# Paged attention, one core: the new-value products of four heads joined into one of 512 columns on a diagonal, and the row maximum taken as a minimum of scaled scores

## The reference

```python
kc = k_cache[block_table].reshape(bsz, L, HK, D)      # 64 sequences, L = 512 cached keys
vc = v_cache[block_table].reshape(bsz, L, HK, D)      # 8 key heads of D = 128
k_all = jnp.concatenate([kc, k], axis=1)              # 32 new tokens behind them
v_all = jnp.concatenate([vc, v], axis=1)
k_all = jnp.repeat(k_all, 4, axis=2)                  # 4 query heads share a key head
v_all = jnp.repeat(v_all, 4, axis=2)
scores = jnp.einsum('bqhd,bkhd->bhqk', q, k_all) * SCALE
scores = jnp.where(valid[:, None, None, :], scores, -1e+30)
probs = jax.nn.softmax(scores, axis=-1)
o = jnp.einsum('bhqk,bkhd->bqhd', probs, v_all)
```

## Time and profile before

| what | value |
|---|---|
| time, median of 3 runs | 3394.45 us (3389.18 to 3395.66) |
| the profiled execution, its own time | 3397.83 us |
| its span, first to last instruction | 3396.0 us |
| mean granted TensorE clock | 0.986 |
| attention stage | about 1630 to 2870 us of the span |

### The profile page before, as it was taken

One profiled execution on the slowest core, in us unless ns is written; L12 is line 12 of the kernel. 1 busy time (PEld: TensorE's weight loads), 2 busy tenths in 40 slices (PEclk: granted clock), 3 DMA queues, 4 the chain that ended last, 5 costly groups with the idle time before them and its releaser, 6 DMA issues. The chain is left out here.

```text
span 3396.0 us, 69875 instructions
## 1 busy us (share of the span) xinstructions
PE 3284.2 (97%) x22398; PEld 3029.0 (89%) x22398; DVE 2326.7 (69%) x6644; ACT 1764.6 (52%) x4307; POOL 1330.0 (39%) x2391
## 2 busy tenths in 40 slices
PE   7799999999899999999899999999999999999999
PEld 5688899987778888888899999999999998888878
DVE  6445544445478787878899999989999996423274
ACT  4323222233327788788666666666666666322222
POOL 0231100000007878888666666656666653100002
PEclk9899999999999999999999999999999999999999
DMA  5422422334545555556766666656666666533353
GB/s 206 135 58 71 127 82 80 86 104 144 199 151 176 173 172 177 183 178 202 238 219 219 213 219 221 219 182 219 214 220 219 222 224 192 178 103 109 115 183 103
DMA packets 448054, 571.96 MB, mean 168 GB/s; under 512 B 171657, under 2 KB 330185, under 8 KB 430794
## 3 DMA queue, kind: packets, MB, share of 16 engines
q1 hardware_dynamic: 427978, 429.08, 40.3%
q0 software_dynamic: 19712, 138.42, 11.6%
HBM read 394.60 MB, written 172.75 MB: 167 GB/s over the span
## 5 line engine op out<-in xcount | busy, mean ns | idle before, releaser
L2625 PE MATMUL l2a_x<-l2a_pt,l2a_V 128*128 128x128 f32 x4096 | 542.3, 275 | 1.0 <-DVE l2a_pn L2559 1.0
L2625 PEld LDWEIGHTS l2a_x<-l2a_pt,l2a_V 128*128 128x128 f32 x4096 | 498.5, 192 | 1.4 <-issue 1.4
L2535 DVE CUSTOM_DVE_ANT_0 l2a_sm<-l2a_s,l2a_B 128x544 f32<-128x544 f32 x512 | 367.9, 719 | 69.3 <-PE l2a_s L197 66.1
L2489 ACT ACTIVATE l2a_p<-l2a_sm,l2a_st 128x544 f32<-128x544 f32 x512 | 380.1, 742 | 27.4 <-DVE l2a_st L2538 27.2
L2344 POOL CAST l2a_K<-cache 128x256 fp32r x768 | 304.2, 447 | 228.6 <-issue 228.6
L2344 POOL CAST keys<-cache 128x256 fp32r x750 | 299.2, 451 | 179.4 <-issue 149.0
L2475 ACT ACTIVATE l2a_pt<-l2a_t 128x512 f32<-128x512 f32 x512 | 305.6, 597 | 101.7 <-PE l2a_t L2608 101.6
L2608 PE MATMUL l2a_t<-ident,l2a_p 128*128 128x128 f32 x2048 | 307.4, 273 | 5.4 <-ACT l2a_ao L2482 5.4
L2549 DVE TENSOR_SCALAR l2a_p<-l2a_p,l2a_st 128x512 f32<-128x512 f32 x512 | 275.6, 538 | 18.2
L2482 ACT ACTIVATE l2a_ao<-l2a_x 128x128 f32<-128x128 f32 x512 | 142.3, 278 | 280.6 <-PE l2a_x L2626 280.5
L197 PE MATMUL l2q_pa<-keys,cache 128*128 128x512 f32 (+1 forms) x1024 | 267.1, 343 | 3.4 <-DVE head L143 3.4
(11 more groups left out here) (856 smaller groups left out, 8672.3 us busy)
## 6 DMA issues: line engine op xcount, KB each, us to landing
s_qT<-l2q_qo SPq DMA_DIRECT2D x128, 512.0 KB, 2.8
head<-s_qT SPq DMA_DIRECT2D x64, 512.0 KB, 5.8
l2a_Q<-s_qT SPq DMA_DIRECT2D x64, 512.0 KB, 5.4
s_ao<-l2a_ao SPq DMA_DIRECT2D x64, 512.0 KB, 6.2
l2o_a<-s_ao SPq DMA_DIRECT2D x128, 256.0 KB, 3.1
s_kn<-l2q_ko SPq DMA_DIRECT2D x128, 128.0 KB, 2.9
head<-s_kn SPq DMA_DIRECT2D x32, 512.0 KB, 5.8
wqraw<-in_wqkv SPq DMA_DIRECT2D x32, 384.0 KB, 3.8
```

The source lines that it names most:

```text
L2489: act.activation(prr[sc % 6][:, :].rearrange("p (k g j) -> p g k j", k=4, j=8), smr[sc % 2][:, :].rearrange("p (g k j) -> p g k j", k=4, j ...
L2535: dve.tensor_tensor_reduce(out=smr[sc % 2][:, :], in0=ps_s[sc % 2][:, 224:768], in1=Br[g % 2][:, :], scale=1.0, scalar=-3e38, op0=ALU.add, ...
L2625: pe.matmul(px[:, P:256], V[:, k * D + hg * P:k * D + hg * P + P], pt[:, k, :], start=k == 0, stop=False)
```

## The change

The new values of a group now land in a plain [128, 128] tile (32 h + s by channel) with no zeros. They are split into a high and a low half `VN` (ScalarE L2513, GpSimd `low_values`). The transposed new probabilities are split too, into `nT` (ScalarE L2501, VectorE L2583). Four DMAs from SBUF to SBUF (`spread`, L2399) then write head h's 32 partitions of `nT` into column block h of `dg`, a tile [128, 2, 512] that is otherwise zero. One joined product in three passes of 512 columns (`mm3` at the group's last turn) adds the new values of all four heads to the `ps_x` bank, which now holds the group's four outputs. ScalarE copies that bank out once a group (L2506). The transposing of `pNr` moves one step later.

On the maximum: the fused VectorE instruction now scales by -SCALE and takes the minimum straight into `s[:, 1:2]`, the bias of the exponential. The separate negation and its semaphore are gone. `new_keys` stands in step `hg == 2` and `mask` in `hg == 3`, where both were in `hg == 2`.

```diff
-    Nr = st.slots("vn", 2, [P, 4, P], each=4)
+    Nr = st.slots("vn", 2, [P, P], each=4)
+    VN = [st.pair(f"vnew{i}", [P, P]) for i in range(2)]
+    nT = st.sb("pnT", [P, 2, P], F32R)
+    dg = st.slots("diag", 1, [P, 2, D], F32R, each=4)
...
+            def spread(g):
+                sp.wait_ge(new_lo, g + 1)
+                if g:
+                    sp.wait_ge(new_mm, g)
...
+                for h in range(4):
+                    at = slice(32 * h, 32 * h + 32)
+                    sp.dma_start(dg[g][at, :, P * h:P * h + P].bitcast(F32), nT[at, :, :].bitcast(F32)).then_inc(dg.sem(g), 16)
...
+                if pv is not None and pv % 4 == 1:
+                    spread(pv // 4)
                 if pv is not None and pv % 8 == 7:
...
-                    sp.wait_ge(o_copied, pv + 1)
+                    sp.wait_ge(o_copied, pv // 4 + 1)
...
+            def low_values(g):
+                pool.wait_ge(values_hi, g + 1)
+                low_part(pool, [z[:, :] for z in VN[g % 2]], Nr[g][:, :]).then_inc(values_lo, 1)
...
+                if hg == 2 and g:
+                    low_values(g - 1)
...
-                    act.activation(ao[k][:, hg, :, 32 * (g % 2):32 * (g % 2) + 32],
-                                   ps_x[pv % 2][:, P:256].rearrange("p (h s) -> p h s", h=4), ACT.Copy).then_inc(o_copied, 1)
+                    if hg == 0:
+                        act.wait_ge(new_turned, g + 1)
...
+                        act.activation(nT[:, 0, :], ps_x[(g + 1) % 2][:, 0:P], ACT.Copy).then_inc(new_hi, 1)
+                    if hg == 3:
+                        act.wait_ge(new_mm, g + 1)
...
+                        act.activation(ao[k][:, :, :, 32 * (g % 2):32 * (g % 2) + 32].rearrange("p g h s -> p (g h) s"),
+                                       ps_x[g % 2][:, :].rearrange("p (h s) -> p h s", s=32), ACT.Copy).then_inc(o_copied, 1)
+                if i % 4 == 0 and 4 <= i <= U:
+                    g = i // 4 - 1
+                    act.wait_ge(*Nr.landed(g))
...
+                    act.activation(VN[g % 2][0][:, :], Nr[g][:, :], ACT.Copy).then_inc(values_hi, 1)
...
-                    dve.tensor_tensor_reduce(out=smr[sc % 2][:, :], in0=ps_s[sc % 2][:, 224:768], in1=Br[g % 2][:, :], scale=1.0,
-                                             scalar=-3e38, op0=ALU.add, op1=ALU.max, accum_out=s[:, 0:1]).then_inc(maxed, 1)
-                    dve.wait_ge(maxed, sc + 1)
-                    dve.tensor_scalar(s[:, 1:2], s[:, 0:1], -SCALE, None, ALU.mult).then_inc(negated, 1)
+                    dve.tensor_tensor_reduce(out=smr[sc % 2][:, :], in0=ps_s[sc % 2][:, 224:768], in1=Br[g % 2][:, :], scale=-SCALE,
+                                             scalar=3e38, op0=ALU.add, op1=ALU.min, accum_out=s[:, 1:2]).then_inc(maxed, 1)
...
+                if pv is not None and pv % 4 == 0:
+                    g = pv // 4
+                    dve.wait_ge(new_hi, g + 1)
+                    dve.tensor_tensor(nT[:, 1, :], ps_x[(g + 1) % 2][:, 0:P], nT[:, 0, :].bitcast(F32), ALU.subtract).then_inc(new_lo, 1)
...
-                    pe.matmul(px[:, P:256], vn[:, hg, :], pnr[g % 2][:, :], start=False, stop=True).then_inc(pv_mm, 1)
...
+                        m = pe.matmul(px[:, P * hg:P * hg + P], V[:, k * D + hg * P:k * D + hg * P + P], pt[:, k, :],
+                                      start=hg + k == 0, stop=False)
+                    m.then_inc(pv_mm, 1)
+                    if hg == 3:
+                        pe.wait_ge(*dg.landed(g))
+                        pe.wait_ge(values_lo, g + 1)
+                        mm3(pe, px[:, :], [([z[:, :] for z in VN[g % 2]], (dg[g][:, 0, :], dg[g][:, 1, :]))], start=False).then_inc(new_mm, 1)
```

More of the change, by code:

```diff
@@ L2306, in l2_attn @@
     ptr = [st.sb(f"pt{i}", [P, 4, P]) for i in range(2)]
-    pnr = [st.sb(f"pn{i}", [P, P]) for i in range(2)]
     str_ = [st.sb(f"st{i}", [P, 8]) for i in range(4)]
@@ L2455, in _ @@
                     page_copies(pool, r, n, range(10, 16), pages_g)
+            low_values(G - 1)
         @block.scalar
@@ L2553, in _ @@
                                       s[:, 3:4], None, ALU.mult).then_inc(newed, 1)
-                if tr is not None and tr % 4 == 0:
-                    g = tr // 4
-                    dve.wait_ge(new_turned, g + 1)
-                    if g >= 2:
-                        dve.wait_ge(pv_mm, 4 * (g - 1))
-                    dve.tensor_copy(pnr[g % 2][:, :], ps_x[tr % 2][:, 0:P]).then_inc(new_copied, 1)
+                if pv is not None and pv % 4 == 0:
+                    g = pv // 4
+                    dve.wait_ge(new_hi, g + 1)
+                    dve.tensor_tensor(nT[:, 1, :], ps_x[(g + 1) % 2][:, 0:P], nT[:, 0, :].bitcast(F32), ALU.subtract).then_inc(new_lo, 1)
                 if sc is not None:
```

57 lines of the change are left out of this document (29 added, 28 removed).

## The result

The changed kernel takes 3602.01 us (median of 4 runs, 3596.10 to 3603.52) against 3393.13 for the kernel before (4 runs, 3389.18 to 3395.66). The ratio is 1.0613, with a 95% interval of 1.0595 to 1.0632. It is slower, as forecast, but by 209 us where 64 were forecast, and outside the range.

A forecast was written before the change was run, and what follows sets the result against it. TensorE was taken as the bound, VectorE second with some 9% spare. From 3397.8 us, minus 24 for the gain, plus 87 for stalls, gave 3461 profiled, 3458 as the median; the range was 3390 to 3545.

The forecast's parts named there:

- the joined product gives 0.19 us a group: TensorE, attention stage: four turns give back 0.89 us, three joined passes cost 0.70; 24 us gained in 128 groups.
- The minimum is neutral: VectorE loses 512 negations and a wait each turn; TensorE covers that, so it counts for nothing.
- groups without a store: Groups after which no store comes: spread at most 2 us late, no stall taken; stalls there would prove the forecast wrong.
- GpSimd's part: One 128 x 128 subtraction a group (`low_values`) into 40% idle time; the forecast is wrong if it ends last.
- ScalarE's wait for the loads: ScalarE waits for the new values (`l2a_vn`) before splitting them, 2 to 3 us in every second group.
- the stall of 1.4 us: TensorE's wait per pair of groups for the late spread: 1.3 from the first path, plus 0.1 for ripples on VectorE.
- hidden after all: Rival, chance 0.13: the spread lands within 7.7 us of the store, TensorE never waits for it, 3370 us.
- T + 8.5: T starts the turn after an odd group's joined product; the next joined product wants to start at T + 8.52.
- 87 for the stalls: Attention stage: 1.4 us for each of 62 stores with a group behind that can be late, 87 us.
- the forecast case: Likeliest case, chance 0.62: a stall of 1.0 to 1.9 us a pair of groups, 3433 to 3489 us.
- Full queue: Rival, chance 0.13: gather ahead of the store holds SP at its next issue, 1.3 us a pair, 81 us, 3539.
- The clock: Rival, chance 0.05: each stall lowers TensorE's clock and loses 1.8 us, 112 us on top, 3570.

The follow-up runs named there:

- e9: Changed kernel with new-value loads first, the transpose of pNr and the spread one turn earlier, and the store behind the spread: 3380.57 us, 0.9955 of the kernel before.
- e3: Kernel before with only the new minimum of scaled scores and no negation: 3392.22 us, 0.9996 of the kernel before.
- e2: Changed kernel with ScalarE's split of the new values three steps later: 3570.43 us, 1.0525 of the kernel before.
- e5: Changed kernel with new-value loads first and the output store two turns later, behind the next group's spread: 3409.06 us, 1.0044 of the kernel before.
- e1: Changed kernel with the loads of new values ahead of the store in SP's queue: 3548.61 us, 1.0464 of the kernel before.
- e16: Changed kernel with every second group's query load bringing 16 of its 128 partitions: 3604.98 us, 1.0616 of the kernel before.
- e13: Changed kernel with the gather waiting for ScalarE's output copy, so issued about with the store: 3572.13 us, 1.0511 of the kernel before.
- e17: Changed kernel with the store as 128 rows of 4 KB and the gather fetching 64 of 128 rows: 3416.61 us, 1.0073 of the kernel before.
- e10: Changed kernel with new-value loads first, the transpose of pNr and the spread one turn earlier, and the store ahead of the spread: 3478.25 us, 1.0258 of the kernel before.
- e11: Changed kernel with the output store written as 128 rows of 4 KB: 3484.73 us, 1.0259 of the kernel before.
- e12: Changed kernel with the gather of cached values fetching 64 of its 128 rows: 3501.93 us, 1.0316 of the kernel before.
- e14: Changed kernel with the gather released one value product, so one turn, later: 3657.36 us, 1.0772 of the kernel before.
- e15: Changed kernel with the query load ahead of the spread in groups that no store precedes: 3703.18 us, 1.0913 of the kernel before.

## Why the prediction was right in direction and wrong in size

**Right.** TensorE was the bound and the joined product gives 0.19 us a group: the groups without a wait take 9.2 us, and e9's stores show 9.2. (Two terms of it were off and cancel: the three passes cost 0.78 us and not 0.70, 2111.50 to 2112.28, and the turn behind them 2.12 and not 2.22.) The minimum is neutral (e3). The spread behind the store is late and TensorE waits for it once in each pair; groups without a store do not wait; GpSimd's part is never last. ScalarE's wait for the loads is there, 4.1 us where 2 to 3 were given, and worth little by itself (e2). Stores are 21.2 us apart in the median, where near 20 were given.

**The step that failed** is the size of one term: "the spread lands behind the new values and about where the query load did: 8.7 to 9.3 after the store", and from it the stall of 1.4 us. The product that waits for it starts 10.2 after the store by the median, and the mean wait is 2.7. I read a landing off another DMA in the old trace, as if the engines' load stayed the same. The runs show that the landing follows from what the engines carry at that time: with the store out of the way the wait goes (e5), lightening store or gather takes 1.07 or 0.95 us off it, both 2.06, and issuing the spread 3.3 us sooner into the same traffic 0.3 (e1). In the old trace DMAs of SP's landed 8.3 and 9.0 after the store beside the same store and gather; the last 1.2 us is new. What the new part is made of stays open, the spread's own 128 KB or the order of the packets; ruled out are the late query load (e16) and, for all but 30 us, the longer issue (e13). The rival "hidden after all" needed a landing by T + 8.5. The last issue alone is near T + 8.0, and the four DMAs of one spread in e13 took 4.0 to 4.6 us from issue to landing.

**Where the 140 us are.** The forecast sum has -24 for the gain and 87 for the stalls, so 63; the spans differ by 203, 140 more: 94 for the stalls, which are 169 us of standing and 12 of restarting where 87 were taken, and 46 for the clock, which the sum had at nothing because the stalls would be short.

**Two rivals came true together with the forecast case.** "Full queue" named the gather ahead of the store and 1.3 us more a pair; the loads' issue did grow by 1.3 us (3.32 to 4.66), and the stall by 1.3. But with the issue back at its old times (e13) 30 us come back, not 81, so the rival's number was right and its mechanism a part of it at most. "The clock" was set at 112 us, with "the stalls are a third as long" against it; at 2.7 us on average they were long enough, behind all of those over 3 us and 9 of the 32 from 2 to 2.5, and it cost 46. Had I let the rivals add, with the clock at what it cost, the sum would have been 3458 + 81 + 46 = 3585, against 3602 measured. Priced as alternatives, each alone stayed inside or near the range and their sum did not.

**Waits cost more than themselves.** From e9 to the changed kernel the waits rise by 167.6 us and the time by 221.4, 1.32 us for each: the clock and the restarts of the sum above. e5, e17, e10, e11, e12, e1, e13, e2 and e16 lie within 10 us of that line. It meets zero waits near 3372 us, where the rival "hidden after all" stood with 3370. e14 and e15, in which groups without a store wait too (119 and 94 waits), lie 28 and 35 us above it.

## What to carry to other kernels

When a change puts a small transfer on the path behind big ones, don't read its landing off another DMA: count the packets that are ahead of it, small ones by their number, and allow for more; and place it ahead of the large store, with a turn of lead, which here (with the loads ahead too) turned a loss of 6% into a gain of 0.5%. Moving it in the issuing queue alone won a quarter of the loss here, mostly from the longest waits, while the engines were full. Rivals that need the same cause (a stall) can all be true at once, so the upper end of a range must hold their sum.

## What the hardware showed that I had not expected

- Issuing can be held up by what is in the queue, and by different amounts: four DMAs of 64 rows each took 2.51 us to issue with nothing small ahead (0.63 each), 7.72 us right behind a store of 2048 packets of 256 bytes (e10); four of 32 rows took 1.82, 3.23 behind the store, 4.66 with the gather ahead too. With the same bytes in 128 packets the loads behind the store took 2.97.
- TensorE's granted clock mostly falls when the stand is over: it was 1.00 over 2131 to 2146, in which TensorE stood 3.82 us, and 0.83 over the next 10 us, in which it was busy throughout. In the two stands over 7 us it fell while TensorE stood (at 1989.1 and 2296.3, where it resumed at 1992.54 and 2300.21). Short stands are not safe: of the 38 of 1 to 2.5 us in that trace 9 had a fall behind them, all of those over 2 us, and in e1 3 of the 27 of 1 to 2 us had one.
- A transfer from SBUF to SBUF of four times 32 KB needed 4.4 us each from issue to landing beside the gather (one pair of e13, median), not far below the 5.0 of a 16 KB load from DRAM in the earlier trace rows.
